# A two-block recurrent kernel on one core: stack clearing moved behind the first norm on GpSimd, the last batch's rounding moved ahead of its maxima on VectorE

## The reference

```python
xn = _layernorm(x)
s = _L0_attn_ref(xn, wq, bq, wk, bk, wv, bv, wo, bo)      # 32 heads of 8, 8 key groups, full softmax
g = _silu(_L0_ffn_ref(xn, ...))                           # two products, then 8 heads that each pick 8 of 2048 experts
x = x + s * g
xn = _layernorm(x)
s = _L1_attn_ref(xn, Wq, Wkv, Wo, bo)                     # 16 heads of 16, 4 key groups, causal, with a linear bias
g = _silu(_L1_ffn_ref(xn, weight, w_scale, bias))         # rows rounded to int8, integer product, scaled
x = x + s * g
```

## Time and profile before

| | us |
|---|---|
| three runs | 785.51, 784.35, 786.27 (median 785.51) |
| the profiled execution, its own time | 787.66 |
| its span from first to last instruction | 785.8 |
| busy: TensorE / VectorE / ScalarE / GpSimd | 528.0 / 592.4 / 255.8 / 514.9 |
| granted TensorE clock, mean | 0.823 of full speed |

### The profile page before, as it was taken

How to read it: one execution, slowest core, us unless ns; L and a number is a source line. 1 busy time by engine, 2 the same in 40 slices (tenths; PEclk the granted TensorE clock), 3 DMA queues, 4 the chain that set the end, 5 groups by cost and what they waited for, 6 DMA issues and landing times.

```text
span 785.8 us, 9193 instructions
## 1 busy us (share of the span) xinstructions
PE 528.0 (67%) x2241; PEld 291.8 (37%) x2258; DVE 592.4 (75%) x2700; ACT 255.8 (33%) x648; POOL 514.9 (66%) x522
## 2 busy tenths in 40 slices
PE   2810466486794567797758558956356996979786
PEld 2600254232373235334336235324233443354432
DVE  4487977797874987799779788869799875775351
ACT  1600151144541112463424114623111473425032
POOL 5077777777775777777777777777777777760000
PEclk9955787788986666899868767978777998989898
DMA  8157565555575555955765555596865559550400
GB/s 292 38 165 220 168 173 155 154 156 155 151 223 162 156 156 165 232 153 153 210 198 159 156 158 160 158 237 186 210 191 153 154 153 256 157 142 1 106 2 15
DMA packets 47765, 125.49 MB, mean 160 GB/s; under 512 B 10715, under 2 KB 20507, under 8 KB 46654
## 3 DMA queue, kind: packets, MB, share of 16 engines
q0 software_dynamic: 32768, 100.70, 45.3%
q1 hardware_dynamic: 14342, 23.90, 10.9%
q10 hardware_dynamic: 600, 0.30, 0.2%
HBM read 119.58 MB, written 4.98 MB: 159 GB/s over the span
## 4 chain that ended last, share of the span: by engine, by line
POOL 50%; issue 18%; PE 13%; DVE 12%; DMA 5%; ACT 1%; POOLq 0%; ACTq 0%; DVEq 0%
POOL rows L551 50%; DMA rows<-experts_table,idx 5%; PE experts L831 3%; DVE hot L1204 3%; DVE acc L1229 2%; PE outs L777 1%; PE experts L839 1%; PE turn L586 1%; PE turn L811 1%; DVE nmax L1245 1%; DVE nmax L1237 1%; PE scores L743 1%; DVE bestp L1129 1%; DVE var L1072 1%; PE turn L807 1%
## 5 line engine op out<-in xcount | busy, mean ns | idle before, releaser
L551 POOL DMA_INDIRECT rows<-experts_table,idx x512 | 505.0, 986 | 188.7 <-issue 151.4
L1204 DVE CUSTOM_DVE_ANT_0 hot<-rows,h 128x128 f32<-128x128 f32 x512 | 114.6, 287 | 108.6 <-DMA rows<-experts_table,idx 108.4
L831 PE MATMUL experts<-rows,diag 128*128 128x256 f32 x384 | 132.4, 497 | 45.4 <-ACT diag L1049 38.2
L683 PE MATMUL turn<-stackk,stackq 125*128 125x256 bf16 x256 | 58.4, 344 | 105.8 <-DVE nmax L1237 52.1
L1229 DVE SCALAR_TENSOR_TENSOR acc<-rows,zs,acc 128x256 f32<-128x256 f32 x304 | 125.7, 478 | 0.9 <-issue 0.3
L831 PEld LDWEIGHTS experts<-rows,diag 128*128 128x128 f32 x384 | 93.3, 254 | 76.5 <-ACT diag L1049 47.0
L997 ACT ACTIVATE probs<-scores 128x512 f32<-128x512 f32 x176 | 97.3, 594 | 59.6 <-PE scores L734 31.1
L1043 ACT ACTIVATE zt<-za 128x8 f32<-128x8 f32 x64 | 13.4, 209 | 259.5 <-DVE za L1208 259.3
L1049 ACT ACTIVATE diag<-ident,zs 128x128 f32<-128x128 f32 x192 | 63.1, 394 | 68.3 <-DVE zs L1214 63.8
L1237 DVE TENSOR_REDUCE nmax<-turn 128x2 f32<-128x512 f32 x128 | 82.2, 682 | 1.8 <-PE turn L683 1.7
L683 PEld LDWEIGHTS turn<-stackk,stackq 125*128 125x128 bf16 x256 | 21.7, 111 | 143.8 <-DVE nmax L1237 78.5
(11 more groups left out here) (156 smaller groups left out, 751.5 us busy)
## 6 DMA issues: line engine op xcount, KB each, us to landing
rows<-experts_table,idx POOLq DMA_INDIRECT x512, 3.2
stackq<-scratchq SPq DMA_DIRECT2D x20, 384.0 KB
scratchq<-parts SPq DMA_DIRECT2D x8, 384.0 KB, 3.2
stackk<-scratchk SPq DMA_DIRECT2D x20, 96.0 KB
xnext<-x SPq DMA_DIRECT2D x4, 256.0 KB, 3.2
wup<-w_wup SPq DMA_DIRECT2D x1, 1024.0 KB, 4.9
slopeq<-c_slopeq SPq DMA_DIRECT2D x1, 1024.0 KB, 5.2
xres<-x SPq DMA_DIRECT2D x4, 256.0 KB, 3.4
```

The lines of the kernel that those rows point to most:

```text
L551: nc.gpsimd.indirect_dma_start(rows[:, slot, c, :], None, tab, bass.IndirectOffsetOnAxis(ap=idx[:, b % 2, t, TOP * h + c:TOP * h + c + 1], ...
L683: ins = mm(ps[:, t * S:(t + 1) * S], stackq[0][r, m, t * P:(t + 1) * P], stackk[0][r, m // QUAD, :], start=True, stop=True)
L831: ins = mm(experts[:, s // FH, :], diag[:, g % 2, k, :], rows[:, g % RING, k, PRIV:ROW], start=(s % FH == 0 and k == 0), stop=(s % FH == F ...
L1204: ins = v.tensor_tensor_reduce(out=zjunk[:, k, :], in0=rows[:, slot, k, 0:PRIV], in1=h2[:, b % 2, t, :], scale=1.0, scalar=0.0, op0=ALU.mu ...
```

## The change

On GpSimd the value tiles are cleared and filled first, GpSimd then waits for the first batch's norm (`xn0_ready`), and the two stacks are cleared behind that, with a semaphore of their own, `stacks_cleared`. SyncE waits for that one where it waited for `cleared`. In VectorE's list `round1:3.0` stands ahead of `max1:3.0` and `max1:3.1` where it stood behind them.

```diff
-    norm1:3.0 split1:3.0 over1:2.0 over1:2.1 fin1:2.0 max1:3.0 max1:3.1 round1:3.0 max1:3.2 max1:3.3 max1:3.4 max1:3.5 max1:3.6
+    norm1:3.0 split1:3.0 over1:2.0 over1:2.1 fin1:2.0 round1:3.0 max1:3.0 max1:3.1 max1:3.2 max1:3.3 max1:3.4 max1:3.5 max1:3.6
...
-        halves, ones_in = sem("halves"), sem("ones_in")
+        halves, ones_in, stacks_cleared = sem("halves"), sem("ones_in"), sem("stacks_cleared")
...
             def load_ones(_, n):
                 r = MAX_AT[0]
-                sp.wait_ge(cleared, 1)
+                sp.wait_ge(stacks_cleared, 1)
...
                 if layer == 0 and b == 0:
-                    sp.wait_ge(cleared, 1)
+                    sp.wait_ge(stacks_cleared, 1)
...
         def _(pool):
-            nc.gpsimd.memset(stackk[0][CLEARED_FROM:P, :, :], 0.0)
-            nc.gpsimd.memset(stackq[0][CLEARED_FROM:P, :, :], 0.0).then_inc(cleared, 1)
-            pool.wait_ge(cleared, 1)
             nc.gpsimd.memset(full(v0), 0.0)
             nc.gpsimd.memset(full(v1), 0.0).then_inc(cleared, 1)
-            pool.wait_ge(cleared, 2)
+            pool.wait_ge(cleared, 1)
             nc.gpsimd.memset(v0one, 1.0)
             nc.gpsimd.memset(v1one, 1.0).then_inc(cleared, 1)
+            pool.wait_ge(cleared, 2)
+            pool.wait_ge(xn0_ready, 1)
+            nc.gpsimd.memset(stackk[0][CLEARED_FROM:P, :, :], 0.0)
+            nc.gpsimd.memset(stackq[0][CLEARED_FROM:P, :, :], 0.0).then_inc(stacks_cleared, 1)
...
                 if b == 0:
                     act.wait_ge(halves, 2)
-                    act.wait_ge(cleared, 3)
+                    act.wait_ge(cleared, 2)
```

## The result

The changed kernel took 783.58 us (median of 20 runs, 781.34 to 786.80) and the kernel before 785.78 (20 runs, 783.71 to 788.89). The ratio is 0.9969, 95% interval 0.9956 to 0.9982: faster by 0.31%, or 2.4 us (1.4 to 3.5); the two medians are 2.2 apart. The forecast was 780.8, 4.7 under before. The direction held, the size was twice too large, and the range (777.3 to 783.8) held by 0.2 us only. The profiled execution took 783.30 us, with a span of 781.5.

The account below looks back on a forecast made before the run. It took three stretches in a row as the bound: a 38 us start, 665 us paced by GpSimd's indirect DMAs, an 83 us tail. Start 2.2 plus tail 2.5 made 4.7 us: 785.5 - 4.7 = 780.8, range 777.3 to 783.8.

Parts of the forecast that it names:

- The stall: Start: `var` and `bits` on VectorE stand behind GpSimd's memsets, 5.56 us together; each should fall to 0.17 us.
- the two loads: Start: ScalarE waits for loads at `identb` (14.27) and `w8b` (22.11), covering 3.4 of the 5.56 us.
- The tail: Last batch's maxima: rounding moves into VectorE's idle time, so twelve maxima run without a gap; gain 2.5 us.
- The gather stage: Indirect DMAs, first to last: stays at 665 us; rival that it swallows the start's gain, 783.0 us, chance 0.05.
- The added wait on GpSimd: Start: GpSimd waits for the norm at about 7.6, then clears stacks until 16.3; claimed to cost nothing.
- the margin of 0.4 us: Start, SyncE: the load of ones, issued at 16.69, waits for the clearing ending at 16.3; 0.4 us are left.
- The step that failed: Start: from `down` to the first expert index everything moves as a block, carrying the 2.2 us gain through.
- the term of 2.2 for the start: Start: `w8b` begins 2.2 us earlier, so `down` starts at 24.3 against 26.53; bounds 0 and 5.56.
- the rival of the clock: TensorE idles ahead of `down`, clock falls to 1.2 GHz, `down` costs 3.7 us more: 784.5 us, chance 0.06.
- The argument against it: Against the clock's fall: a 2.3 us tail stretch with 0.10 us of matmul left the clock at 1.00.
- the load at 22.1: Start: the loads through `maskT` land at 22.11; `w8b` needs them ahead of the fourth part of `up`.

Follow-up runs that it names:

- e1: Kernel before with only the rounding (`round1:3.0`) moved ahead of the maxima: 785.46 us, ratio 0.9964 against the kernel before.
- e2: Kernel before with only the stack clearing moved, VectorE's list as before: 788.42 us, ratio 0.9994 against the kernel before.
- e5: The whole change again, unchanged, on a third, slower chip: runs of 952 to 992 us, no ratio on record.
- e9: The whole change a third time, unchanged, on the second chip: 785.07 us, ratio 0.9956 against the kernel before.
- e6: Kernel before with only the conversion `w8b` moved behind `fold` on ScalarE, on the slower third chip: ratio 1.0000 against the kernel before.
- e7: Kernel before with stack clearing moved and `w8b` behind `fold`, rounding left where it was, on the slower third chip: ratio 1.0014.
- e10: Same kernel as e7 (stack clearing and `w8b` moved, rounding not), on the second chip: 784.70 us, ratio 0.9944 against the kernel before.
- e3: Whole change plus five matmuls without a result on TensorE between `fold` and `down`: 783.44 us, ratio 0.9946 against the kernel before.
- e4: Whole change plus `w8b` moved on ScalarE from ahead of the fourth part of `up` to behind `fold`: 778.90 us, ratio 0.9880 against the kernel before.
- e11: Same kernel as e6 (only `w8b` moved behind `fold`), on the second chip: 788.83 us, ratio 1.0008 against the kernel before.
- e12: Kernel of e4 plus 6, 4 and 2 warm matmuls in TensorE's three idle tail stretches, second chip: 779.33 us, ratio 0.9888 against the kernel before.

## Why the prediction was wrong

**Right, step by step.** The stall was GpSimd's clearing: `var` and `bits` went to 0.17 us in every kernel with the clearing moved. What became late next were the two loads, at 14.0 (14.27 forecast) and 22.0 (22.11), so that `down` started at 24.16 (24.3). The tail gave 2.5 us in three profiles and 2.8 by the runs of e1. The gather stage kept its length within its own spread (663 to 669 us in ten profiles on these chips), so that an earlier first DMA was an earlier last one. The added wait on GpSimd cost nothing: the clearing ended at 16.56 (9.64 + 6.92), and the load of ones was issued at 16.59. There the margin of 0.4 us was in truth none, since SyncE came to it sooner than before.

**The step that failed** is this sentence of the start: "From `down` to the first index everything is one after another and is moved as a block." The order was right, the durations were not. The sum took `down` at its 3.70 us, and so put the fall of the clock at nothing. In the four profiles of kernels that have the gap ahead of it (2.1 to 3.8 us long), it took 5.38 (the change), 5.33 (e2), 5.38 (e5) and 6.29 (e9); in the ten without a gap 3.69 to 3.72. So the term of 2.2 for the start measured 0.7 in the change and in e2, 1.0 in e5 (against e6 on the same chip) and -0.7 in e9; by the runs of e2 it is 0.5, between -1.4 and 2.4. 2.5 from the tail and about nothing from the start make the 2.4 that were measured.

That was the rival of the clock. It stood in the prediction with the right place and a price of up to 3.7 (measured 1.6 to 2.6), and got a chance of 0.06. It put TensorE's idle time at "1 to 2 us". The times of the kernel before give more. Its timeline has `fold` here:

```profile
24.60 1.99 PE L606 MATMUL turn<-rows 64*128 64x45 f32 x32
```

That is 9.6 us behind the start of `up`, and `down` begins 1.93 later. So with `up` at 9.94 `fold` is done at 21.5, and `down` at 24.3 comes 2.8 behind it. Measured were 2.37. The argument against it failed too: "in the tail a stretch of 2.3 us with 0.10 of matmul left the clock at 1.00". That was one look at one execution. In e7 and e10 the same stretch, of the same length, was followed by a fall. Whether the clock holds behind such a gap can't be read off a single passage. The prediction also cited the Trainium skill (TensorE: Matmul & The Clock Gate, What's actually happening), whose rule is that recent activity sets the clock. The traces agree: in e3 the same 2.4 us with matmuls in them kept it at 1.00.

**Two waits, one behind the other.** The prediction counted the load at 22.1 as a cap on the gain, which it was, but not as the cause of a gap. Removing the first wait turned a stage in which TensorE was busy without a break (up, fold, down at 15.0 to 30.2 us) into one with a hole, and the hole cost what was left of the gain. Taking the second wait out as well gave both back: 9.4 us for e4 against 2.4 to 3.5 for the change. Its profiled execution is 787.66 - 777.28 = 10.4 below that of before: 5.4 in the start, 1.1 in the gather stage, 2.5 in the tail by the rounding and 1.7 by the clock in the last projection, less 0.3 between the last DMA and the first maximum. That last 1.7 (in the projection and in the bias products just ahead of it) is not shown to be e4's own. The profiles of e3 and e4 had it, those of the change, e1 and e9 did not, and two executions of one kernel, on two chips, differed: in e6 the projection took 1.89 us, in e11 3.02. What decides it stays open. The forecast's range held with some luck: it was drawn around two gains, and one of them hardly came.

## What to carry to other kernels

When a stall is removed ahead of a stage that keeps TensorE busy, work out where it will stand idle next, and price the matmuls behind that gap at the low clock as well as at the high one, unless the gap is closed. A wait in another engine's list (here a conversion whose result is first read at 312.5 us, 290 later) can be free for as long as a longer one stands ahead of it, and should be moved together with that one. Work out the length of the gap from the rows, too, and not by eye. One passage of a trace in which the clock held is no evidence that it holds.

## What the runs showed of the hardware

A VectorE `TENSOR_SCALAR` on 128x2 numbers stood for 5.04 us behind a GpSimd memset and ended within 0.03 us of it. A `SCALAR_TENSOR_TENSOR` with two inputs in SBUF ran beside the same memset, in the changed kernel, at its usual 0.69 us (15.89 to 16.58, while the clearing ran to 16.56). The Trainium skill (SBUF — State Buffer, Who interferes with whom) says as much, that two inputs contend only with a GpSimd instruction that reads, and this row agrees.

The granted clock fell behind gaps of 2.1 to 3.8 us in some passages (four of four ahead of `down`, the 2.3 in the tails of e7 and e10) and not in others (the 2.3 in the tails of the kernel before, e2, e6 and e11). The fall could land inside the matmuls that follow (25.5 in the changed kernel) or ahead of all of them (e9). Ahead of the last projection, where TensorE's idle times were 0.70, 1.06 and 0.75 us with 1.1 and 0.7 us of matmuls between them, the clock fell in eight profiles of twelve. The runs of e4 (six within 2.8 us) and e12 (six within 1.6) lay closer than the twelve of e10 (10.9), but those of e3, without the gap, were spread over 6.1 us and those of e9, with it, over 4.6, so that a link of gaps and spread is not shown.

One of the chips ran all kernels at 982 us. Most of the difference lay in the gather stage (830 to 859 us), where GpSimd in e6 waited 90.0 us for TensorE's sums and 57.2 us for VectorE's, against 8.1 and 1.5 in the profile of the kernel before. Another 15 to 24 us were added between the last indirect DMA and the first maximum. Why was not looked into.
